# When GpSimd weighs two tiles of an expert layer: after a fixed pair step of the scans, or as soon as they are centred

## The chip, the core and the metric

One core of a Trainium2 chip runs the whole program. The metric is the time of one execution on the device, in microseconds (us); less is better. Five engines work side by side, each on its own list of instructions in order: TensorE (PE: matrix products and transposes), VectorE (DVE), ScalarE (ACT), GpSimd (POOL) and the queue of SyncE (SP), which starts transfers. They wait for one another through semaphores only. GpSimd starts the indirect transfers (gathers) too.

## What is computed

The program is two layers of a recurrent model. The part that matters here is the first: on the same normed input, a Mamba block (a scan over 512 positions) and a mixture of 24 experts with two choices for each token. The experts' first product is combined, layer-normed, passed through a relu, and goes into the experts' second product.

```
# Mamba: 8 sequences of 512, 256 channels, 16 states
h = dA * h + dBx          # a scan along the sequence, for each of 16 states
y = sum over states of h * C
# experts: W1 is 128 to 512, W2 512 to 128
h = moe_apply(xf, combine, dispatch, W1, b1)
h = layer_norm(h, lw, lb)   # lw, lb: one vector of 512 for each of 4 groups
h = relu(h)
return moe_apply(h, combine, dispatch, W2, b2)
```

## The kernel before, in words

Tokens lie in 32 tiles of 128 rows. The scan stage runs the Mamba scans as main work and the experts' work beside it: on each engine a function (side_by_side) takes a piece of the main list and then a piece of the other in turn, so the order of both on an engine is fixed when the program is written.

Main work: 64 pair steps, numbered 0 to 63, eight for each of eight sequences. Pair step i treats two states of 256 channels. TensorE spreads rows of B and C over 128 partitions in PSUM (L653, tile sc_p_bc). VectorE then does four products of 128x1024, two with B (L783) and two with C for the step before (L793); each has one input in SBUF and one in PSUM. Then it does two scans (L811, tensor_tensor_scan, 128x1024), whose two inputs, the decays sc_dA and the states sc_st, both lie in SBUF; each scan adds one to the semaphore scanned. Position q = i mod 8 in a sequence decides some extra work: at q = 3 and q = 6 the scans are followed by four short operations of the softplus for the next sequence (L760, L763, L764, L766, 128x512), whose inputs lie in SBUF, and the last adds one to u_ready. ScalarE makes the decays (L596), TensorE sums the states (L684).

Beside it, in steps 22 to 42, the combination of the first expert layer is done, two tiles (one unit u of 16) for each pair step:

- GpSimd gathers two rows of the experts' first product for each token of a tile: two gathers a tile (L1434, into the buffer yk of four tiles). The gather of tile t waits until tile t-4 has been combined (semaphore biased).
- TensorE adds a bias (L1528) and the two gathered rows (L1532) in a PSUM bank of two.
- ScalarE copies the bank out (L1655), works out mean and variance in a number of small instructions, and in its turn for unit u centres and scales unit u-2 (L1643, buffer ro of six tiles; semaphore centred) after it did the relu of unit u-4 (L1636), which waits for GpSimd.
- GpSimd weighs a unit: it multiplies the two centred tiles (128x1024) with the norm's weight (L1454) and adds the norm's bias (L1456), both in SBUF (semaphore weighted). All stands in one list: the gathers of tiles 2u+2 and 2u+3, then the weighing of unit u-3, and so on. The gathers come to an end with tile 31; units 12 to 15 are weighed without gathers between them.
- SyncE stores each unit after the relu, and when all is stored GpSimd gathers for the second expert layer (L1464).

Two waits stand ahead of a weighing: centred, and that of wait_window: unit u is weighed after the scans of pair step 25+u (scanned at 2 * (26+u)), or, where that step is at q = 3 or 6, after the softplus behind its scans (u_ready).

Of the kernel before, what the change touches and what calls it, by code (L numbers as in the profile page):

```python
# [29 lines left out]
DI, DS, DTR, KC = 256, 16, 8, 4  # L30
# [175 lines left out]
def front_stage(nc, w, src_dram, xn_dram, x_rows, xn_rows, xnT, xT, z, pt, routing, early, late, first,  # L206
# [3 lines left out]
    with ExitStack() as ctx:  # L210
# [74 lines left out]
        @block.gpsimd  # L285
        def _(pool):
            pool.wait_ge(stored, 16 * B)
            pool.wait_ge(turned, B)
            nc.gpsimd.memset(zero_rows, 0.0).then_inc(zeroed, 1)
            pool.wait_ge(routing.tab_ready, 1)  # L290
            pool.wait_ge(gates_stored, 16)
            for e in range(Moe0Experts.AHEAD):
                for h in range(HG):
                    nc.gpsimd.indirect_dma_start(
                        out=xg[:, e, h, :], out_offset=None, in_=xn_dram.rearrange("p t d -> (p t) d"),
                        in_offset=bass.IndirectOffsetOnAxis(ap=r.tab[:, h, e:e + 1], axis=0),
                    ).then_inc(gathered1[e], 16)
# [185 lines left out]
EVEN_FROM, EVEN_TO, FIRST_WINDOW = 22, 43, 26  # L483
# [7 lines left out]
def scan_stage(nc, w, xT, z, spare, first, beside):  # L491
# [6 lines left out]
    with ExitStack() as ctx:  # L498
# [338 lines left out]
        @block.gpsimd  # L837
        def _(pool):
            for _ in beside.pool(pool):
                pass  # L840
# [465 lines left out]
class Moe0Experts:  # L1306
# [108 lines left out]
    def pool(self, pool):  # L1415
        nc, r = self.nc, self.r

        def gather_x(e):
            if e >= E0:
                return  # L1420
            if e >= 4:
                pool.wait_ge(self.piece_read, 5 * (e - 3))
            for h in range(HG):
                nc.gpsimd.indirect_dma_start(  # L1424
                    out=self.xg[:, e % 4, h, :], out_offset=None, in_=self.xn_rows,
                    in_offset=bass.IndirectOffsetOnAxis(ap=r.tab[:, h, e:e + 1], axis=0),
                ).then_inc(self.gathered1[e % 4], 16)

        def gather_y(u):
            for t in range(2 * u, min(2 * u + 2, NT)):  # L1430
                if t >= 4:
                    pool.wait_ge(self.biased, t - 3)
                for k in range(2):
                    nc.gpsimd.indirect_dma_start(  # L1434
                        out=self.yk[:, t % 4, k, :], out_offset=None, in_=self.y1_rows,
                        in_offset=bass.IndirectOffsetOnAxis(ap=r.back[:, k, t:t + 1], axis=0),
                    ).then_inc(self.gathered_y[t % 4], 16)

        def wait_window(i):

            b, q = divmod(i - 1, DS // 2)
            if q in (3, 6):
                pool.wait_ge(self.u_ready, 2 * (b + 1) + (q - 3) // 3 + 1)
            else:
                pool.wait_ge(self.scanned, 2 * i)

        def weigh(u):

            pool.wait_ge(self.centred, 2 * u + 2)
            wait_window(FIRST_WINDOW + u)  # L1450
            t = 2 * u
            ro = self.ro[:, t % 6:t % 6 + 2, :]
            g = slice(t % HG, t % HG + 2)
            nc.gpsimd.tensor_tensor(ro, ro, self.w["ln_w"][:, g, :], ALU.mult).then_inc(self.p_chain, 1)  # L1454
            pool.wait_ge(self.p_chain, u + 1)
            nc.gpsimd.tensor_tensor(ro, ro, self.w["ln_b"][:, g, :], ALU.add).then_inc(self.weighted, 1)  # L1456

        def gather_r(e):
            if e >= E0:
                return  # L1460
            if e >= 3:
                pool.wait_ge(self.turned2, HG * (e - 2))
            for h in range(HG):
                nc.gpsimd.indirect_dma_start(  # L1464
                    out=self.rg[:, e % 3, h, :], out_offset=None, in_=self.r_rows,
                    in_offset=bass.IndirectOffsetOnAxis(ap=r.tab[:, h, e:e + 1], axis=0),
                ).then_inc(self.gathered2[e % 3], 16)

        for e in range(E0):
            gather_x(e + self.AHEAD)  # L1470
            yield
        for i in range(2):
            pool.wait_ge(self.stored1[i], 16 * (E0 // 2))
        gather_y(0)
        yield
        for u in range(self.UNITS + 4):
            gather_y(u + 1)
            if 3 <= u < self.UNITS + 3:
                weigh(u - 3)
            yield  # L1480
        for i in range(3):
            pool.wait_ge(self.stored_r[i], 16 * len(range(i, self.UNITS, 3)))
        for e in range(self.AHEAD):
            gather_r(e)
        yield
        for e in range(E0):
            gather_r(e + self.AHEAD)
            yield
# [1529 lines left out]
```

## Time and profile before

| | us |
|---|---|
| median of 3 runs | 1442.43 (1440.59 to 1442.75) |
| the profiled execution | 1438.98 |
| its span, first to last instruction | 1436.1 |
| scans of the first layer (L811), first to last start | 108.4 to 772.6 |
| units weighed (L1454), first to last start | 371.8 to 551.3 |

Busy time over the whole span: TensorE 1258.3 us (88%), VectorE 1199.1 (83%), ScalarE 883.8 (62%), GpSimd 681.2 (47%). These are means over stages of different kinds; for this change the stretch from 360 to 560 us counts. All times in this text are us from the start of the span. The timeline lists an engine's instructions by start, duration and, in brackets, the idle time of the engine ahead of it and what ended it. A duration includes time in which the instruction was held up after its start.

### The profile page before, as it was taken

The page shows a single profiled execution, that of the slowest core. Times are in us where ns is not written, and L with a number is a line of the kernel's source. Part 1 is how long each engine was busy: PE and PEld are TensorE (multiplying, and loading weights), DVE is VectorE, ACT ScalarE, POOL GpSimd, SP SyncE. Part 2 cuts the span into 40 slices and gives each one's busy share as a digit, 9 for nine tenths or more (in the row PEclk, how much of TensorE's full clock was granted, in tenths as well). Part 3 has the DMA queues.
Part 4 walks back from the last instruction along what each step waited for, and adds up shares of the span by engine and source line. Part 5 has one row for each costly group of instructions (what it writes and reads, how often), then busy time and mean ns, then how long its engine had stood idle before and what let it go on. Part 6 is the DMA issues. An engine that isn't in the chain of part 4 may idle for free. (4 is left out here: it accounts for less than half of the span.)

```text
span 1436.1 us, 21390 instructions
## 1 busy us (share of the span) xinstructions
PE 1258.3 (88%) x7254; PEld 874.3 (61%) x7260; DVE 1199.1 (83%) x2410; ACT 883.8 (62%) x2114; POOL 681.2 (47%) x633
## 2 busy tenths in 40 slices
PE   6988798887988865999897997799999999999997
PEld 5444354443443433888896775467667777777775
DVE  6868999998888889999996778688898755568876
ACT  5577667575988885556553657756456444544462
POOL 0026565615688855655651775338640143146300
PEclk9999999999889977999998899899999999999999
DMA  8014555455233422445552721010002044213200
GB/s 257 1 24 114 144 144 155 130 142 150 90 107 128 133 74 84 136 138 142 163 146 61 235 53 37 15 42 4 1 2 59 7 111 127 62 33 49 28 29 31
DMA packets 86021, 128.82 MB, mean 90 GB/s; under 512 B 15488, under 2 KB 50657, under 8 KB 85306
## 3 DMA queue, kind: packets, MB, share of 16 engines
q1 hardware_dynamic: 66458, 75.70, 18.0%
q0 software_dynamic: 19456, 51.77, 14.0%
q8 instruction: 58, 0.95, 0.3%
q14 instruction: 49, 0.40, 0.1%
HBM read 86.66 MB, written 40.77 MB: 89 GB/s over the span
## 5 line engine op out<-in xcount | busy, mean ns | idle before, releaser
L811 DVE TENSOR_TENSOR_SCAN sc_st<-sc_dA,sc_st 128x1024 f32<-128x1024 f32 x128 | 291.0, 2317 | 0.0
L2359 DVE COPY at_pT<-at_p_t 128x512 f32<-128x512 f32 (+1 forms) x192 | 108.8, 599 | 105.2 <-PE at_p_t L2136 105.0
L793 DVE TENSOR_TENSOR sc_st<-sc_st,sc_p_bc 128x1024 f32<-128x1024 f32 x128 | 155.7, 1217 | 31.6 <-PE sc_p_bc L653 31.5
L596 ACT ACTIVATE sc_dA<-sc_dt,g_state 128x511 f32<-128x511 f32 x256 | 168.8, 709 | 6.2 <-DVE sc_st L811 5.5
L783 DVE TENSOR_TENSOR sc_st<-sc_u,sc_p_bc 128x1024 f32<-128x1024 f32 x128 | 155.1, 1212 | 7.5 <-PE sc_p_y L684 6.5
L1464 POOL DMA_INDIRECT g_state<-r_scratch,moe_tab x96 | 122.2, 1273 | 82.0 <-PE e_bank L1560 55.2
L1424 POOL DMA_INDIRECT g_state<-xn_scratch,moe_tab x88 | 117.5, 1335 | 84.3 <-ACT g_state L1584 48.1
L2232 ACT ACTIVATE at_pr<-at_pr,at_nmx 128x512 f32<-128x512 f32 (+3 forms) x256 | 140.2, 552 | 23.3 <-DVE at_nmx L2318 23.2
L2116 PE MATMUL at_p_s<-g_xT,at_qT 128*128 128x512 f32 (+3 forms) x512 | 149.4, 435 | 0.0
L653 PE MATMUL sc_p_bc<-sc_bc,mamba_sel 96*128 96x512 bf16 x256 | 102.4, 401 | 51.3 <-DVE sc_st L783 47.4
L684 PEld LDWEIGHTS sc_p_y<-g_ident,sc_st 128*128 128x128 f32 x1024 | 121.7, 144 | 27.5 <-issue 14.1
L684 PE MATMUL sc_p_y<-g_ident,sc_st 128*128 128x128 f32 x1024 | 136.1, 277 | 2.0 <-DVE sc_st L793 1.9
L1434 POOL DMA_INDIRECT g_state<-y_scratch,moe_back x64 | 93.1, 1455 | 56.8 <-DMA y_scratch<-g_state 32.3
L2318 DVE CUSTOM_DVE_ANT_0 at_pr<-at_p_s,l_mask_wide 128x512 f32<-128x512 f32 (+3 forms) x256 | 110.4, 486 | 6.0 <-PE at_p_s L2116 5.5
L2116 PEld LDWEIGHTS at_p_s<-g_xT,at_qT 128*128 128x128 f32 x512 | 83.0, 191 | 50.2 <-issue 32.1
L1513 PE MATMUL e_bank<-g_state 128*96 128x512 f32 x192 | 99.0, 614 | 10.7 <-ACT g_state L1574 10.6
L1547 PE MATMUL e_bank<-g_state 128*96 128x128 f32 x768 | 101.7, 276 | 4.4 <-ACT g_state L1675 4.0
L1584 ACT ACTIVATE g_state<-e_bank,g_state 96x512 f32<-96x512 f32 x96 | 65.0, 680 | 62.1 <-PE e_bank L1513 60.3
L2136 PEld LDWEIGHTS at_p_t<-g_ident,at_pr 128*128 128x128 f32 x640 | 74.8, 141 | 43.0 <-DVE at_pT L2359 31.5
L2136 PE MATMUL at_p_t<-g_ident,at_pr 128*128 128x128 f32 x640 | 91.6, 274 | 6.9 <-DVE at_pT L2359 6.0
L1684 ACT ACTIVATE g_state<-e_bank 128x384 f32<-128x384 f32 x96 | 46.8, 487 | 77.7 <-PE e_bank L1560 77.6
L2570 POOL DMA_INDIRECT f_m<-y_scratch,l_back x64 | 60.4, 943 | 71.7 <-DMA y_scratch<-f_out 33.4
(343 smaller groups left out, 2718.9 us busy)
## 6 DMA issues: line engine op xcount, KB each, us to landing
y_scratch<-g_state SPq DMA_DIRECT2D x24, 768.0 KB, 5.2
g_state<-W SPq DMA_DIRECT2D x48, 256.0 KB, 5.5
r_scratch<-g_state SPq DMA_DIRECT2D x16, 512.0 KB, 2.6
y_scratch<-g_state SPq DMA_DIRECT2D x24, 192.0 KB, 2.7
xn_scratch<-g_state SPq DMA_DIRECT2D x16, 256.0 KB, 4.2
g_state<-x SPq DMA_DIRECT2D x4, 512.0 KB, 7.0
g_state<-xn_scratch SPq DMA_DIRECT2D x8, 256.0 KB, 5.8
g_state<-x SPq DMA_DIRECT2D x1, 2048.0 KB
```

Source lines behind the costliest of these rows:

```text
L596: ins = nc.scalar.activation(dA[:, m % 4, j, 1:L], dt[:, b % 2, h, 1:L], ACT.Exp, scale=negA[:, h, 2 * q + j:2 * q + j + 1])
L684: ins = nc.tensor.matmul(p_y[:, t, h * P:(h + 1) * P], st[:, m + h, j, t * P:(t + 1) * P], w["ident"], is_transpose=True, start=False, sto ...
L783: nc.vector.tensor_tensor(st[:, m % RS:m % RS + 2, j, :], u[:, b % 2, :, :], p_bc[:, k % 3, :].unsqueeze(1).broadcast_to([P, HALF, L]), AL ...
L793: nc.vector.tensor_tensor(states, states, p_bc[:, k % 3, :].unsqueeze(1).broadcast_to([P, HALF, L]), ALU.mult).then_inc(row_used, 1)
L811: nc.vector.tensor_tensor_scan(st[:, m % RS, :, :].rearrange("p a b -> p (a b)"), dA[:, m % 4, :, :].rearrange("p a b -> p (a b)"), st[:, ...
L1424: nc.gpsimd.indirect_dma_start(out=self.xg[:, e % 4, h, :], out_offset=None, in_=self.xn_rows, in_offset=bass.IndirectOffsetOnAxis(ap=r.ta ...
L1464: nc.gpsimd.indirect_dma_start(out=self.rg[:, e % 3, h, :], out_offset=None, in_=self.r_rows, in_offset=bass.IndirectOffsetOnAxis(ap=r.tab ...
L2116: ins = nc.tensor.matmul(p_s[:, bank, c:c + K], qT[:, n % 3, i * P:(i + 1) * P], xaT[:, b, 0:K], start=True, stop=True)
L2136: ins = nc.tensor.transpose(p_t[:, bank, c + (i - j) * P:c + (i - j + 1) * P], pr[:, n % 3, sbank, sc + j * P:sc + (j + 1) * P], w["ident"])
L2232: ins = nc.scalar.activation(row, row, ACT.Exp, scale=-1.0, bias=nmx[:, n % 2, i:i + 1], accum_out=sums[:, n % 4, i:i + 1])
L2318: ins = v.tensor_tensor_reduce(out=pr[:, n % 3, bank, c:c + K], in0=p_s[:, bank, c:c + K], in1=w["mask_wide"][:, L - K:L], scale=1.0, scal ...
L2359: v.tensor_copy(pT[:, n % 2, part, 0:cols], p_t[:, PT_BANK[part], 0:cols]).then_inc(pT_ready, 1)
```

## The change

The function wait_window and its call in weigh are taken away. Nothing else is changed: no instruction, no order.

```
-        def wait_window(i):
-
-            b, q = divmod(i - 1, DS // 2)
-            if q in (3, 6):
-                pool.wait_ge(self.u_ready, 2 * (b + 1) + (q - 3) // 3 + 1)
-            else:
-                pool.wait_ge(self.scanned, 2 * i)
-
         def weigh(u):
 
             pool.wait_ge(self.centred, 2 * u + 2)
-            wait_window(FIRST_WINDOW + u)
             t = 2 * u
```

GpSimd's list before, at the gathers of one unit and the two weighings around them (g_state is the arena in which ro and yk lie, e_ the expert part, sc_ the scan part):

```order
L1454 TENSOR_TENSOR g_state<-g_state,moe_ln_w 128x1024 [waits sc_scanned,e_centred]
L1456 TENSOR_TENSOR g_state<-g_state,moe_ln_b 128x1024 [waits e_p_chain]
L1434 DMA g_state<-y_scratch,moe_back 128x512 [waits e_biased]
L1434 DMA g_state<-y_scratch,moe_back 128x512
L1434 DMA g_state<-y_scratch,moe_back 128x512 [waits e_biased]
L1434 DMA g_state<-y_scratch,moe_back 128x512
L1454 TENSOR_TENSOR g_state<-g_state,moe_ln_w 128x1024 [waits sc_u_ready,e_centred]
L1456 TENSOR_TENSOR g_state<-g_state,moe_ln_b 128x1024 [waits e_p_chain]
```

And in the changed kernel, where all lines behind are nine less:

```order
L1445 TENSOR_TENSOR g_state<-g_state,moe_ln_w 128x1024 [waits e_centred]
L1447 TENSOR_TENSOR g_state<-g_state,moe_ln_b 128x1024 [waits e_p_chain]
L1434 DMA g_state<-y_scratch,moe_back 128x512 [waits e_biased]
L1434 DMA g_state<-y_scratch,moe_back 128x512
L1434 DMA g_state<-y_scratch,moe_back 128x512 [waits e_biased]
L1434 DMA g_state<-y_scratch,moe_back 128x512
L1445 TENSOR_TENSOR g_state<-g_state,moe_ln_w 128x1024 [waits e_centred]
L1447 TENSOR_TENSOR g_state<-g_state,moe_ln_b 128x1024 [waits e_p_chain]
```

The order is the same; the waits for sc_scanned and sc_u_ready are gone from the multiplication, and e_centred and, on the gathers, e_biased are left.

GpSimd's list before, at the last gather and the units 12 to 14, which follow one another:

```order
L1434 DMA g_state<-y_scratch,moe_back 128x512
L1454 TENSOR_TENSOR g_state<-g_state,moe_ln_w 128x1024 [waits sc_scanned,e_centred]
L1456 TENSOR_TENSOR g_state<-g_state,moe_ln_b 128x1024 [waits e_p_chain]
L1454 TENSOR_TENSOR g_state<-g_state,moe_ln_w 128x1024 [waits sc_scanned,e_centred]
L1456 TENSOR_TENSOR g_state<-g_state,moe_ln_b 128x1024 [waits e_p_chain]
L1454 TENSOR_TENSOR g_state<-g_state,moe_ln_w 128x1024 [waits sc_u_ready,e_centred]
L1456 TENSOR_TENSOR g_state<-g_state,moe_ln_b 128x1024 [waits e_p_chain]
```

And in the changed kernel:

```order
L1434 DMA g_state<-y_scratch,moe_back 128x512
L1445 TENSOR_TENSOR g_state<-g_state,moe_ln_w 128x1024 [waits e_centred]
L1447 TENSOR_TENSOR g_state<-g_state,moe_ln_b 128x1024 [waits e_p_chain]
L1445 TENSOR_TENSOR g_state<-g_state,moe_ln_w 128x1024 [waits e_centred]
L1447 TENSOR_TENSOR g_state<-g_state,moe_ln_b 128x1024 [waits e_p_chain]
L1445 TENSOR_TENSOR g_state<-g_state,moe_ln_w 128x1024 [waits e_centred]
L1447 TENSOR_TENSOR g_state<-g_state,moe_ln_b 128x1024 [waits e_p_chain]
```

Here no gather stands between two weighings, so that only e_centred parts them.

## Rows read from the trace of the kernel before

**Rows 1.** Busy time by stretch, columns: stretch, length, each engine, PEclk, DMA.

```profile
385.00:515.00 130.00, 110.72 (x363) 51.23 (x362) 104.91 (x76) 113.97 (x311) 116.07 (x62) 0.87 0.40 125
515.00:560.00 45.00, 27.17 (x119) 17.29 (x118) 44.06 (x33) 31.85 (x69) 18.87 (x9) 0.77 0.15 59
560.00:780.00 220.00, 198.77 (x1683) 178.44 (x1682) 216.20 (x157) 126.16 (x233) 122.20 (x96) 0.98 0.49 133
```

**Rows 2.** Timeline of GpSimd, one round: start, us, operation, idle before.

```profile
440.72 2.79 POOL L1434 DMA_INDIRECT g_state<-y_scratch,moe_back  x1 [0.15 <-issue]
443.81 1.84 POOL L1434 DMA_INDIRECT g_state<-y_scratch,moe_back  x1 [0.30 <-issue]
...
447.21 0.95 POOL L1434 DMA_INDIRECT g_state<-y_scratch,moe_back  x1 [0.30 <-issue]
448.17 2.36 POOL L1454 TENSOR_TENSOR g_state<-g_state,moe_ln_w 128x1024 f32<-128x1024 f32 x1
450.61 2.35 POOL L1456 TENSOR_TENSOR g_state<-g_state,moe_ln_b 128x1024 f32<-128x1024 f32 x1
453.10 2.91 POOL L1434 DMA_INDIRECT g_state<-y_scratch,moe_back  x1
```

**Rows 3.** Groups by line, 360 to 560 us: busy, mean ns, idle before, releasers.

```profile
L811 DVE TENSOR_TENSOR_SCAN sc_st<-sc_dA,sc_st 128x1024 f32<-128x1024 f32 x35 | 83.1, 2413 | 0.0
...
L793 DVE TENSOR_TENSOR sc_st<-sc_st,sc_p_bc 128x1024 f32<-128x1024 f32 x34 | 41.3, 1214 | 21.6 <-PE sc_p_bc L653 21.6
...
L783 DVE TENSOR_TENSOR sc_st<-sc_u,sc_p_bc 128x1024 f32<-128x1024 f32 x34 | 41.1, 1210 | 4.2 <-PE sc_p_y L684 4.2
...
L1454 POOL TENSOR_TENSOR g_state<-g_state,moe_ln_w 128x1024 f32<-128x1024 f32 x16 | 38.2, 2387 | 34.3 <-DVE sc_st L811 24.1 <-DVE sc_u L766 10.1
...
L1636 ACT ACTIVATE g_state<-g_state 128x1024 f32<-128x1024 f32 x16 | 16.9, 1053 | 26.1 <-POOL g_state L1456 26.1
```

**Rows 4.** Timeline of GpSimd: the first two tiles weighed.

```profile
371.80 2.79 POOL L1454 TENSOR_TENSOR g_state<-g_state,moe_ln_w 128x1024 f32<-128x1024 f32 x1 [10.01 <-DVE sc_st L811]
```

**Rows 5.** Timeline of VectorE: scans of steps 26, 28, 37 (x2 merges two), a wait.

```profile
376.92 4.46 DVE L811 TENSOR_TENSOR_SCAN sc_st<-sc_dA,sc_st 128x1024 f32<-128x1024 f32 x2
...
388.81 1.22 DVE L793 TENSOR_TENSOR sc_st<-sc_st,sc_p_bc 128x1024 f32<-128x1024 f32 x1 [4.05 <-PE sc_p_bc L653]
...
403.20 4.47 DVE L811 TENSOR_TENSOR_SCAN sc_st<-sc_dA,sc_st 128x1024 f32<-128x1024 f32 x2
...
515.54 4.47 DVE L811 TENSOR_TENSOR_SCAN sc_st<-sc_dA,sc_st 128x1024 f32<-128x1024 f32 x2
```

**Rows 6.** Timelines of GpSimd and VectorE: a weighing beside scans of step 29.

```profile
412.13 4.38 POOL L1456 TENSOR_TENSOR g_state<-g_state,moe_ln_b 128x1024 f32<-128x1024 f32 x1
...
412.09 6.58 DVE L811 TENSOR_TENSOR_SCAN sc_st<-sc_dA,sc_st 128x1024 f32<-128x1024 f32 x2
```

**Rows 7.** Timelines of VectorE and GpSimd in the next stage: short two-input operations.

```profile
873.65 1.37 DVE L1844 TENSOR_TENSOR g_xT<-g_xT,g_state 128x256 f32<-128x256 f32 x1
...
877.63 0.43 DVE L1844 TENSOR_TENSOR g_xT<-g_xT,g_state 128x256 f32<-128x256 f32 x1
...
873.43 1.31 POOL L1791 TENSOR_TENSOR g_xT<-g_xT 128x512 f32<-128x512 f32 x1
```

**Rows 8.** Timeline of GpSimd: units 12 and 13, without gathers.

```profile
520.15 2.35 POOL L1454 TENSOR_TENSOR g_state<-g_state,moe_ln_w 128x1024 f32<-128x1024 f32 x1 [5.11 <-DVE sc_st L811]
...
532.74 2.36 POOL L1454 TENSOR_TENSOR g_state<-g_state,moe_ln_w 128x1024 f32<-128x1024 f32 x1 [7.81 <-DVE sc_u L766]
```

**Rows 9.** Timeline of VectorE: scans of step 38 and the softplus behind them.

```profile
525.37 4.47 DVE L811 TENSOR_TENSOR_SCAN sc_st<-sc_dA,sc_st 128x1024 f32<-128x1024 f32 x2
529.75 0.67 DVE L760 SCALAR_TENSOR_TENSOR g_state<-g_state,sc_logs 128x512 f32<-128x512 f32 x1
```

**Rows 10.** Timeline of ScalarE: centring of unit 14, and its wait for unit 13.

```profile
526.49 1.50 ACT L1643 ACTIVATE g_state<-g_state,e_nm,e_rstd 128x512 f32<-128x512 f32 x2
...
537.56 1.06 ACT L1636 ACTIVATE g_state<-g_state 128x1024 f32<-128x1024 f32 x1 [4.07 <-POOL g_state L1456]
```

## The prediction

> **What bounds the kernel now.** I read the busy times by stretch first, since the shares over the whole span mix stages. From 560 to 780 us VectorE is busy 216.2 of 220 us, from 515 to 560 it is busy 44.06 of 45; from 385 to 515 only 104.91 of 130, while GpSimd is busy 116.07 and ScalarE 113.97 [rows 1]. So VectorE's scans pace the stage, except in the stretch where gathers and weighings share GpSimd. There one round of GpSimd is four gathers and a weighing, without a gap: from the gather at 440.72 to that at 453.10 are 12.38 us [rows 2]. VectorE's steps keep the same pace: from the scans of step 26 at 376.92 to those of step 37 at 515.54 are 138.62 us for 11 steps, 12.60 each [rows 5]. What GpSimd is late with reaches VectorE through TensorE and ScalarE: VectorE waits 21.6 us ahead of L793 and 4.2 us ahead of L783, and ScalarE waits 26.1 us for weighings ahead of its relu [rows 3]. The waits removed are the two releasers of L1454, 24.1 and 10.1 us, in 8 of its 16 instructions [rows 3]; the first alone is 10.01 us, from 361.79 to 371.80 [rows 4].
>
> **What the wait did beside waiting.** Scans and weighings hold each other up. At 412.13 the second operation of a weighing took 4.38 us instead of 2.35, and the two scans that began at 412.09 took 6.58 instead of 4.47 [rows 2, 5, 6]: the first scan ran 2.2 us, then the weighing 2.35 while the second scan stood, then the second scan. So a weighing operation that comes while the first scan runs costs VectorE 2.1 to 2.35 us, one that comes in the second scan costs it nothing, and one that is under way when the first scan wants to begin costs the rest of itself. Short operations with both inputs in SBUF suffer alike: a TENSOR_TENSOR of 128x256 took 1.37 us beside a GpSimd operation of the same kind that began at 873.43 and took 1.31, and 0.43 alone [rows 7]. The four products of a step, with one input in PSUM, are not held: their mean over the whole stretch with its weighings is 1.21 us [rows 3]. The gathers are held too, but hold nobody: 2.79 and 1.84 us beside scans, 0.95 alone [rows 2], and the scans beside them stay at 4.46 or 4.47 [rows 5].
>
> The last point is where a page speaks otherwise. The Trainium skill (SBUF — State Buffer, Who interferes with whom) says that a VectorE tensor_tensor with two SBUF inputs contends with GpSimd's reads and infers that the making of DMA descriptors is not held by it. By that a round of GpSimd would be 2.73 us shorter (1.84 and 0.89 less), 9.65 us, and GpSimd would not be the bound before. The trace disagrees, if a scan counts as such an instruction, and I go by the rows.
>
> **The sum, part by part.** No instruction goes or comes, so everything lies in when weighings run. Behind the multiplication in GpSimd's list stand the addition and the next unit's gathers; who waits for these are ScalarE's relu and TensorE's L1532.
>
> *1. Removed waits, steps 26 to 37.* The first weighing begins at 361.79 instead of 371.80 (its tiles were centred long before: the wait named is the scans), and later ones lose the short waits for softplus. The two long waits of these last units, 5.11 and 7.81 us [rows 8], are not in this part. At best GpSimd ends its last gather 10.0 us earlier, and some 2 us more for three short waits inside the rounds (10.1 - 7.81 = 2.3 [rows 3, 8]): a bound of -12.3 us, if no collision is added.
>
> *2. Added collisions, steps 26 to 37.* I walk the first rounds. A weighing from 361.8 to 366.7, four gathers in 7.4 us beside the scans of step 25, then the next weighing from 374.2 to 379.0 (two operations at 2.44, 2.35 each). The scans of step 26, wanted at 376.92, start at 379.0: 2.1 lost. They end at 383.4; the four products take 4.5, so step 27 wants its scans at 387.9. GpSimd's gathers, held by the scans, end at 386.6, its first operation runs to 389.0: 1.1 lost; the first scan runs to 391.3, the second operation to 393.6, the second scan stands 2.35. Then softplus and products lead to 403.2, where the next weighing is in its second half, to 405.4: 2.2 lost. Three steps have lost 7.75 us, 2.6 a step, and the wait of 4.05 at 388.81 and a shorter one are gone. Step 28's scans, at 403.20 before, come at 405.4. Over the twelve steps 26 to 37 that is 12 x 2.6 = 31 us, against the 25.8 us of waits (21.6 + 4.2) and the collisions that before has already (83.1 us for 35 scans [rows 3], where 35 of 4.47 / 2 are 78.2: 4.9), together 30.7. I take **0** for parts 1 and 2 together. The bounds: -12.3 as above, and +8 if the kernel falls into the pattern that alternates at every step: products, half a weighing waited for (1.75), scan, weighing (2.35), scan, which is 9.0 + 4.1 = 13.1 a step against 12.6, so 6 us in 11 steps and the 2 of the start. I stay near the middle, since the walk of three rounds is the nearest that I have.
>
> *3. The tail, units 12 to 15.* Before, each waited for its window, 5.11, 7.81 and 9.0 us for the last two (24.1 - 10.01 - 5.11) [rows 3, 4, 8], and cost VectorE at most 0.4. Here VectorE is the bound with nothing to win, and nothing slows GpSimd: 4.9 us a unit. Unit 12 follows unit 11 at about 515: its first operation comes between the scans of step 37, +2.35. Unit 13 starts near 524.8, its first half holds the first scan of step 38 by 0.4 and its second half comes between the two scans, +2.35; the wait of 0.8 that stood ahead of step 38 goes. Unit 14, whose tiles are centred by 528.0 [rows 10], comes in the second scan and then beside the softplus behind step 38. Its four short operations, 0.7 us each [rows 9], need one another in turn, so GpSimd can take its turn ahead of each: two operations of unit 14 and two of unit 15, 4 x 2.35 = +9.4. Unit 15 is there for it, since the centring of 15 stood behind a relu that waited 4.07 us for unit 13 [rows 10], and that now is weighed by 532. Sum: 2.35 + 0.4 - 0.8 + 2.35 + 9.4 = **+13.7 us**. What is least sure is the 9.4: no row shows four such turns in a row, only the one of rows 7. From below it is 0 (the softplus done before unit 14 gets in), from above 9.4.
>
> Behind step 38 no weighing is left to collide, the lateness stays: VectorE has 3.8 us of air in the 220 us to the stage's end [rows 1], and the next stage starts when this one ends. Total 0 + 13.7 = +13.7 us, on the profiled execution 1438.98 + 13.7 = 1452.7. The median of the runs before is 3.45 us above that execution, so 1442.43 + 13.7 = **1456.1 us**.
>
> **The rivals.**
> - *The change as walked, tail and all*: 1456, from 1450 to 1464 (the pattern of every step adds 8). For it: each single collision has its row. Against it: the times of the tail depend on ScalarE's turn to 1 or 2 us. Chance 0.58.
> - *The tail misses the softplus*: ScalarE centres 15 later, or unit 14 is through before. Then 2.35 + 0.4 - 0.8 + 2.35 = +4.3, 1446.7, with part 2 at 0 to +3. Chance 0.16.
> - *Faster: GpSimd's head start is kept.* The mechanism is the round: GpSimd is the one without a gap, and collisions cost VectorE time that it had spare anyway, as long as they stay under 25.8 us in the twelve steps, 2.15 a step. If they come to 1.5 a step, GpSimd's 12.3 are kept in large part: about -12 in these steps, +4.3 in the tail, -8: 1434.7. ScalarE's own work allows it (113.97 busy in 130 us, so 11.0 a step). Chance 0.16.
> - *Nothing changes*: half of the weighings (8 of 16) did not wait for the window at all [rows 3], and the others might find their phase by themselves, since the gathers are held by the scans and so put the weighing behind them. Then within 3 us of 1442.4. Chance 0.10.
>
> **How the numbers follow.** 0.2% is 2.9 us, about what a measurement of this kernel can tell from no change. Slower: 0.58, most of the second rival (0.15), together 0.74. Same: 0.10. Faster: 0.16. The range leaves out the faster rival's better half and the worst pattern at every step together with a full tail: 1437 to 1465.
>
> **What would show it.** In the changed kernel L1454 waits for no scan; its first instruction starts near 361.8. The scans (L811) have a sum about 30 us above 83.1 in the stretch, with pairs of 6.6 to 8 us instead of 4.47. VectorE's 21.6 us ahead of L793 shrink below 12, and ScalarE's 26.1 below 8. The scans of step 37 start within some us of 515.5, those of step 39 about 14 us after 537; L760 to L766 behind step 38 take 10 to 12 us in all. It would be wrong if step 37 came by 508 already, if the scans kept 4.47 beside weighings, or if the lateness at 560 shrank by the stage's end.

## The result, and the profile after

| | before | changed |
|---|---|---|
| median, us | 1442.59 (1440.59 to 1445.08, 4 runs) | 1459.15 (1457.42 to 1460.3, 4 runs) |
| ratio to before | | 1.0114, 95% interval 1.0088 to 1.0141 |
| span of the profiled execution | 1436.1 | 1457.4 |

The changed kernel is slower by 16.6 us, 1.1%. Of the 21.3 us between the two profiled spans not all belongs to the change: the scans of step 24, ahead of the first weighing, begin at 356.56 in the one trace and at 360.78 in the other, and in the traces of the experiments below at 360.1 to 362.6. So I compare traces by the time since the scans of step 24: to those of step 37, with which the rounds of gathers end, and to those of step 42, behind which both kernels run the same way.

| us from the scans of step 24 | before | changed | difference |
|---|---|---|---|
| to step 37 | 158.98 | 167.95 | +9.0 |
| to step 42 | 210.46 | 228.16 | +17.7 |

The busy times by stretch, in the changed kernel (columns: stretch, length, TensorE, its weight loads, VectorE, ScalarE, GpSimd, clock, DMA share):

```profile
385.00:515.00 130.00, 106.02 (x329) 49.04 (x327) 128.75 (x72) 109.11 (x299) 118.49 (x59) 0.84 0.38 118
515.00:575.00 60.00, 32.16 (x131) 17.91 (x130) 59.90 (x36) 35.93 (x84) 34.48 (x11) 0.76 0.12 44
575.00:795.00 220.00, 200.24 (x1667) 178.87 (x1667) 218.05 (x159) 127.82 (x234) 125.24 (x96) 0.96 0.49 135
```

VectorE is busy 128.75 of 130 us between 385 and 515, against 104.91 before [rows 1]: it has no idle time left, and yet is slower. What fills it is time in which its instructions are held. The groups by line show that, from 360 to 575 us:

```profile
L811 DVE TENSOR_TENSOR_SCAN sc_st<-sc_dA,sc_st 128x1024 f32<-128x1024 f32 x34 | 118.1, 3513 | 0.0
...
L1447 POOL TENSOR_TENSOR g_state<-g_state,moe_ln_b 128x1024 f32<-128x1024 f32 x16 | 62.7, 3916 | 1.3
...
L1445 POOL TENSOR_TENSOR g_state<-g_state,moe_ln_w 128x1024 f32<-128x1024 f32 x16 | 42.5, 2654 | 4.4 <-ACT g_state L1634 4.1
L793 DVE TENSOR_TENSOR sc_st<-sc_st,sc_p_bc 128x1024 f32<-128x1024 f32 x34 | 41.2, 1211 | 0.0
L783 DVE TENSOR_TENSOR sc_st<-sc_u,sc_p_bc 128x1024 f32<-128x1024 f32 x33 | 39.9, 1208 | 0.9 <-PE sc_p_y L684 0.9
...
L1627 ACT ACTIVATE g_state<-g_state 128x1024 f32<-128x1024 f32 x16 | 16.7, 1045 | 0.9 <-POOL g_state L1447 0.8
```

The waits of before are gone: 21.6 us ahead of L793 are 0, the 4.2 us ahead of L783 are 0.9, and the 26.1 us that ScalarE waited for weighings are 0.8 [rows 3]. In their place the 34 scans take 118.1 us, 3513 ns each, where 35 took 83.1 and 2413 ns (rows 3 are of 360 to 560 us). GpSimd's second operation (L1447, the old L1456) takes 3916 ns in the mean.

The pattern of the rounds, on both engines. GpSimd first, then VectorE, start and duration in front:

```profile
366.11 2.38 POOL L1445 TENSOR_TENSOR g_state<-g_state,moe_ln_w 128x1024 f32<-128x1024 f32 x1
...
380.41 2.38 POOL L1445 TENSOR_TENSOR g_state<-g_state,moe_ln_w 128x1024 f32<-128x1024 f32 x1
...
393.81 2.36 POOL L1445 TENSOR_TENSOR g_state<-g_state,moe_ln_w 128x1024 f32<-128x1024 f32 x1
396.25 4.23 POOL L1447 TENSOR_TENSOR g_state<-g_state,moe_ln_b 128x1024 f32<-128x1024 f32 x1
...
409.91 4.34 POOL L1447 TENSOR_TENSOR g_state<-g_state,moe_ln_b 128x1024 f32<-128x1024 f32 x1
```

```profile
381.14 8.11 DVE L811 TENSOR_TENSOR_SCAN sc_st<-sc_dA,sc_st 128x1024 f32<-128x1024 f32 x2
...
393.67 8.96 DVE L811 TENSOR_TENSOR_SCAN sc_st<-sc_dA,sc_st 128x1024 f32<-128x1024 f32 x2
402.55 0.66 DVE L760 SCALAR_TENSOR_TENSOR g_state<-g_state,sc_logs 128x512 f32<-128x512 f32 x1
...
409.82 6.58 DVE L811 TENSOR_TENSOR_SCAN sc_st<-sc_dA,sc_st 128x1024 f32<-128x1024 f32 x2
```

The first weighing stands at 366.11 with no wait ahead of it, 5.3 us after the scans of step 24 (before: 15.2). The pair of scans of step 27 takes 8.96 us instead of 4.47. The start of the first scan is recorded 0.14 us before that of GpSimd's multiplication, and yet the multiplication takes 2.36 us, as alone, and the pair takes two of GpSimd's operations longer: multiplication, scan, addition (4.23 us, held by the scan), scan. The next pair starts 16.15 us later, behind the softplus, at 409.82, together with GpSimd's addition, and takes 6.58 us. From step 26 to step 37 the pairs come 13.42 us apart in the mean, and GpSimd's multiplications of units 1 to 11 (380.41 to 515.37) 13.50 us. Between 385 and 515 us GpSimd waits 1.1 us for another engine and VectorE 0.9, so the two meet again at every step: of the twelve pairs none takes under 6.5 us, and four take 8.96.

The tail, GpSimd and then VectorE:

```profile
530.17 3.04 POOL L1445 TENSOR_TENSOR g_state<-g_state,moe_ln_w 128x1024 f32<-128x1024 f32 x1 [1.25 <-ACT g_state L1634]
533.29 4.22 POOL L1447 TENSOR_TENSOR g_state<-g_state,moe_ln_b 128x1024 f32<-128x1024 f32 x1
540.34 3.86 POOL L1445 TENSOR_TENSOR g_state<-g_state,moe_ln_w 128x1024 f32<-128x1024 f32 x1 [2.83 <-ACT g_state L1634]
544.27 4.21 POOL L1447 TENSOR_TENSOR g_state<-g_state,moe_ln_b 128x1024 f32<-128x1024 f32 x1
548.44 2.79 POOL L1445 TENSOR_TENSOR g_state<-g_state,moe_ln_w 128x1024 f32<-128x1024 f32 x1
551.31 2.67 POOL L1447 TENSOR_TENSOR g_state<-g_state,moe_ln_b 128x1024 f32<-128x1024 f32 x1
```

```profile
528.73 6.62 DVE L811 TENSOR_TENSOR_SCAN sc_st<-sc_dA,sc_st 128x1024 f32<-128x1024 f32 x2
...
539.79 6.56 DVE L811 TENSOR_TENSOR_SCAN sc_st<-sc_dA,sc_st 128x1024 f32<-128x1024 f32 x2
546.27 2.76 DVE L760 SCALAR_TENSOR_TENSOR g_state<-g_state,sc_logs 128x512 f32<-128x512 f32 x1
549.07 2.71 DVE L763 TENSOR_TENSOR g_state<-sc_logs,g_state 128x512 f32<-128x512 f32 x1
551.81 2.71 DVE L764 TENSOR_TENSOR sc_dt<-sc_dt,g_state 128x512 f32<-128x512 f32 x1
554.56 0.69 DVE L766 TENSOR_TENSOR sc_u<-sc_dt,g_xT 128x512 f32<-128x512 f32 x1
...
559.69 4.47 DVE L811 TENSOR_TENSOR_SCAN sc_st<-sc_dA,sc_st 128x1024 f32<-128x1024 f32 x2
```

The pairs of steps 37 and 38 take 6.62 and 6.56 us. Three of the four short softplus operations behind step 38 take 2.7 to 2.8 us instead of 0.69, each ending about 0.55 us behind one of GpSimd's operations of units 14 and 15, so that it ran when that had ended; the fourth is alone.

### The profile page after: what moved, and what is told of

It reads as the page before. It is cut to its first block and busy times, and to the rows that moved or that the text cites. A ratio compares the mean times of both kernels' runs of the same rounds, so it can differ in the third digit from the quotient of the medians.

```text
span 1457.4 us, 21380 instructions
## 1 busy us (share of the span) xinstructions
PE 1266.4 (87%) x7260; PEld 878.6 (60%) x7260; DVE 1241.6 (85%) x2410; ACT 883.8 (61%) x2114; POOL 708.6 (49%) x633
## 5 line engine op out<-in xcount | busy, mean ns | idle before, releaser
L811 DVE TENSOR_TENSOR_SCAN sc_st<-sc_dA,sc_st 128x1024 f32<-128x1024 f32 x128 | 328.2, 2607 | 0.0
L596 ACT ACTIVATE sc_dA<-sc_dt,g_state 128x511 f32<-128x511 f32 x256 | 169.1, 710 | 19.3 <-DVE sc_st L811 11.8
L653 PE MATMUL sc_p_bc<-sc_bc,mamba_sel 96*128 96x512 bf16 x256 | 103.4, 405 | 87.1 <-DVE sc_st L783 83.1
L1455 POOL DMA_INDIRECT g_state<-r_scratch,moe_tab x96 | 125.2, 1305 | 102.7 <-PE e_bank L1551 54.9
L793 DVE TENSOR_TENSOR sc_st<-sc_st,sc_p_bc 128x1024 f32<-128x1024 f32 x128 | 155.5, 1216 | 9.6 <-PE sc_p_bc L653 9.5
L783 DVE TENSOR_TENSOR sc_st<-sc_u,sc_p_bc 128x1024 f32<-128x1024 f32 x128 | 155.0, 1211 | 5.1 <-PE sc_p_y L684 3.2
L1434 POOL DMA_INDIRECT g_state<-y_scratch,moe_back x64 | 89.6, 1400 | 56.9 <-DMA y_scratch<-g_state 32.4
L1504 PE MATMUL e_bank<-g_state 128*96 128x512 f32 x192 | 99.9, 620 | 12.3 <-ACT g_state L1565 12.2
L653 PEld LDWEIGHTS sc_p_bc<-sc_bc,mamba_sel 96*128 96x128 bf16 x256 | 25.9, 101 | 129.7 <-DVE sc_st L783 106.3
```

What stands on the lines that cost most here:

```text
L596: ins = nc.scalar.activation(dA[:, m % 4, j, 1:L], dt[:, b % 2, h, 1:L], ACT.Exp, scale=negA[:, h, 2 * q + j:2 * q + j + 1])
L653: nc.tensor.matmul(p_bc[:, k % 3, :], w["sel"][:, n * P:(n + 1) * P], bc3[:, b % 2, :], start=True, stop=True).then_inc(row_ready, 1)
L783: nc.vector.tensor_tensor(st[:, m % RS:m % RS + 2, j, :], u[:, b % 2, :, :], p_bc[:, k % 3, :].unsqueeze(1).broadcast_to([P, HALF, L]), AL ...
L793: nc.vector.tensor_tensor(states, states, p_bc[:, k % 3, :].unsqueeze(1).broadcast_to([P, HALF, L]), ALU.mult).then_inc(row_used, 1)
L811: nc.vector.tensor_tensor_scan(st[:, m % RS, :, :].rearrange("p a b -> p (a b)"), dA[:, m % 4, :, :].rearrange("p a b -> p (a b)"), st[:, ...
L1455: nc.gpsimd.indirect_dma_start(out=self.rg[:, e % 3, h, :], out_offset=None, in_=self.r_rows, in_offset=bass.IndirectOffsetOnAxis(ap=r.tab ...
```

## The experiments

The theory: the loss is that a GpSimd operation reading SBUF and a VectorE instruction with two inputs there exclude each other, so that the removed wait's worth was to keep weighings beside the four products. Against it stand, part by part: that all of the loss is in the tail (my sum), that it is GpSimd's time or the order of its work, and that it comes from the head start alone. The wait's condition is changed in six kernels, the weighing itself in two. The table gives each run's measured ratio, the difference of the medians and, from its one trace, the time since step 24 against before. Where a ratio is turned into us below, it is taken of the median before; the differences of the medians are up to 2.2 us away from that. Two traces of the same kernel (first_free) are 4.7 us apart at step 37, so a difference of a few us between two traces shows nothing by itself.

| kernel | units that wait | median, us | ratio to before, 95% | medians' difference | to step 37 | to step 42 |
|---|---|---|---|---|---|---|
| changed | none | 1459.15 | 1.0114 (1.0088 to 1.0141) | +16.6 | +9.0 | +17.7 |
| tail_kept | 12 to 15 | 1450.84 | 1.0051 (1.0032 to 1.0070) | +9.4 | +8.9 | +8.4 |
| tail_free | 0 to 11 | 1452.41 | 1.0061 (1.0040 to 1.0082) | +10.9 | -1.1 | +10.7 |
| first_kept | 0 | 1450.00 | 1.0046 (1.0025 to 1.0067) | +8.5 | -5.3 | +6.7 |
| first_free | 1 to 15 | 1437.71 | 0.9967 (0.9945 to 0.9988) | -3.8 | -7.9 | -7.1 |
| first_free_again | 1 to 15 | 1437.65 | 0.9963 (0.9941 to 0.9984) | -5.2 | -3.2 | -3.6 |
| middle_free | 0, 12 to 15 | 1439.32 | 0.9983 (0.9964 to 1.0002) | -2.7 | -4.9 | -4.1 |
| second_kept | 1, 12 to 15 | 1436.35 | 0.9963 (0.9937 to 0.9988) | -6.5 | -8.8 | -8.1 |
| softplus_kept | 2, 5, 10, 13 | 1444.97 | 1.0017 (0.9999 to 1.0036) | +3.0 | -1.2 | +5.6 |
| write_only | none, reads nothing | 1420.78 | 0.9865 (0.9836 to 0.9894) | -21.2 | -22.0 | -20.3 |
| no_weighing | no weighing | 1422.71 | 0.9869 (0.9840 to 0.9897) | -19.3 | -22.1 | -20.3 |

The kernel before ran beside each group: 1441.47 us (the first four experiments), 1441.99 (the next four in time: write_only, no_weighing, softplus_kept, middle_free), 1442.88 (the last two).

### Where the loss lies: rounds or tail

```
-            wait_window(FIRST_WINDOW + u)
+            if u >= 12:
+                wait_window(FIRST_WINDOW + u)
```

> The wait for the pair step is kept for units 12 to 15 and gone for units 0 to 11. My theory after the changed kernel's trace: the twelve steps with gathers cost 9 us of the 16.6, because scans and weighings alternate at 13.4 us a step instead of 12.6; so this is 9 us above the kernel before, near 1451.6 us. The rival, my own sum on record: these steps cost nothing (0) and all of it lies in the tail; then it equals the kernel before, 1442.6 us.

Measured: 0.51% above before, 7.4 us. Step 37 is reached as late as in the changed kernel, and from there nothing more is lost. VectorE's scans of steps 35 to 38 show the switch, two pairs beside weighings without wait and two behind them:

```profile
501.37 8.94 DVE L811 TENSOR_TENSOR_SCAN sc_st<-sc_dA,sc_st 128x1024 f32<-128x1024 f32 x2
...
517.51 6.58 DVE L811 TENSOR_TENSOR_SCAN sc_st<-sc_dA,sc_st 128x1024 f32<-128x1024 f32 x2
...
528.52 4.46 DVE L811 TENSOR_TENSOR_SCAN sc_st<-sc_dA,sc_st 128x1024 f32<-128x1024 f32 x2
...
537.41 4.85 DVE L811 TENSOR_TENSOR_SCAN sc_st<-sc_dA,sc_st 128x1024 f32<-128x1024 f32 x2
```

```
+            if u < 12:
+                wait_window(FIRST_WINDOW + u)
```

> The wait is kept for units 0 to 11 and gone for units 12 to 15. Theory: the tail costs 7 to 9 us, mostly by four short softplus operations behind step 38 that each wait for a weighing operation, so about 1450.5 us. My sum on record said 13.7 us, 1456.3. Rival: with units 0 to 11 at their old times, unit 15 does not meet the softplus and the tail costs only the scans' 4.3 us, 1446.9.

Measured: 0.61%, 8.8 us. Within what was measured the two parts add up: by the ratios 7.4 + 8.8 = 16.2 us against 16.6 for both, by the medians 9.4 + 10.9 = 20.3, by the traces at step 42 8.4 + 10.7 = 19.1 against 17.7; the intervals are 4.6 to 10.1 and 5.8 to 11.8 us. By the trace the tail is 11.8 us (10.7 + 1.1), more than in the changed kernel, because here all four softplus operations are held, one by each operation of units 14 and 15, 2.05 us each:

```profile
532.54 6.58 DVE L811 TENSOR_TENSOR_SCAN sc_st<-sc_dA,sc_st 128x1024 f32<-128x1024 f32 x2
539.03 2.77 DVE L760 SCALAR_TENSOR_TENSOR g_state<-g_state,sc_logs 128x512 f32<-128x512 f32 x1
541.83 2.71 DVE L763 TENSOR_TENSOR g_state<-sc_logs,g_state 128x512 f32<-128x512 f32 x1
544.58 2.71 DVE L764 TENSOR_TENSOR sc_dt<-sc_dt,g_state 128x512 f32<-128x512 f32 x1
547.33 2.72 DVE L766 TENSOR_TENSOR sc_u<-sc_dt,g_xT 128x512 f32<-128x512 f32 x1
549.96 1.21 DVE L783 TENSOR_TENSOR sc_st<-sc_u,sc_p_bc 128x1024 f32<-128x1024 f32 x1
```

The rival, that unit 15 misses the softplus, is refuted, and so is my sum's 0 for the rounds.

### Is it the head start

```
+            if u == 0:
+                wait_window(FIRST_WINDOW + u)
```

> Only unit 0 waits for its pair step, all others are free. Two theories on why steps 26 to 37 lose 9 us. If it is the head start of 10 us that puts GpSimd's rounds into the wrong phase, this kernel keeps the rhythm of before (8 of 16 weighings did not wait there anyway), loses only the tail's 8 us, and takes about 1450.5 us. If the alternating pattern draws every rhythm in that has no wait, it is as slow as the changed kernel, 1459 us.

Measured: 0.46%, 6.6 us, so not the 16.6 of the changed kernel: the alternating pattern does not draw in every rhythm. With one wait at the start the rounds reach step 37 even 5.3 us earlier than before, and the tail then loses 12.0. So the 9 us in the rounds come from the phase that the unwaited first weighing sets, together with the waits that are missing later: each alone does not bring them. Two kernels further on in the table narrow this down to a single wait each. middle_free is tail_kept with the wait of unit 0, and takes 1439.32 us where tail_kept took 1450.84; second_kept is tail_kept with the wait of unit 1, and takes 1436.35.

```
+            if u > 0:
+                wait_window(FIRST_WINDOW + u)
```

> Only unit 0 is free, units 1 to 15 keep the wait. Unit 0 fits between the gathers of tile 9 and the scans of step 25, where it collides with nothing, and the four gathers behind it come 10 us earlier; unit 1 then waits for step 26 and starts at its window, some 3.3 us earlier than in the kernel before (381.4 instead of 384.66). Theory: 3 us faster than before, 1439.6 us, since GpSimd's round of 12.4 us is the bound up to the last gather. Rival: the head start is lost at the first window, and the time is that of before, 1442.6.

Measured: 0.33% faster, and 0.37% in a second run of the same kernel. GpSimd's timeline shows the first weighing where the changed kernel has it, and the second at its window:

```profile
366.05 2.37 POOL L1455 TENSOR_TENSOR g_state<-g_state,moe_ln_w 128x1024 f32<-128x1024 f32 x1
...
385.69 2.36 POOL L1455 TENSOR_TENSOR g_state<-g_state,moe_ln_w 128x1024 f32<-128x1024 f32 x1 [5.36 <-DVE sc_st L811]
```

> The kernel in which only unit 0 is free, once more: it was 0.33% faster than the kernel before, with an interval from 0.12% to 0.55%. If the reason holds (the round of GpSimd is the bound up to the last gather, and its first weighing meets no scan), it is 0.2 to 0.5% faster again, 1435 to 1439 us; if it was chance, it equals the kernel before.

The rival is refuted: the head start is kept by the wait of unit 1, not lost there. The two traces differ (7.9 and 3.2 us at step 37), so a part of the gain depends on the execution. In the first of them GpSimd waits for VectorE only once between 385 and 515 us, those 5.36 us of unit 1: the waits of units 2 to 11 stand in the list and are always met already. In the second unit 5 waits 2.15 us and unit 10 0.78.

### Is it the reading of SBUF

```
-            nc.gpsimd.tensor_tensor(ro, ro, self.w["ln_w"][:, g, :], ALU.mult).then_inc(self.p_chain, 1)
-            pool.wait_ge(self.p_chain, u + 1)
-            nc.gpsimd.tensor_tensor(ro, ro, self.w["ln_b"][:, g, :], ALU.add).then_inc(self.weighted, 1)
+            for k in range(3):
+                nc.gpsimd.memset(ro, 0.5).then_inc(self.p_chain, 1)
+                pool.wait_ge(self.p_chain, 3 * u + k + 1)
+            nc.gpsimd.memset(ro, 0.5).then_inc(self.weighted, 1)
```

> The changed kernel, with each weighing (a multiplication and an addition that read and write 128x1024 in SBUF) replaced by four memsets of the same two tiles, which write SBUF and read nothing; so the norm's weight and bias of the first expert layer are left out and the relu's input is a constant. GpSimd is busy about as long. Theory: the loss is the reading of SBUF by GpSimd beside operations of VectorE with two inputs there; then the pairs of scans go back to about 4.5 us and the softplus operations to 0.7, and the time falls to 1435 to 1440 us. Rival: what is lost is GpSimd's time and order, or its writes hold the scans as well; then pairs of 6.6 to 9 us stay and the time is 1450 us or more.

Measured: 1.35% faster than before, 19.5 us, below what I expected. The groups by line, 355 to 575 us, and the stretch of the rounds:

```profile
L811 DVE TENSOR_TENSOR_SCAN sc_st<-sc_dA,sc_st 128x1024 f32<-128x1024 f32 x43 | 96.0, 2271 | 0.0
...
L1446 POOL MEMSET g_state<- 128x1024 f32 x48 | 45.9, 956 | 22.1 <-ACT g_state L1635 20.2
...
L1448 POOL MEMSET g_state<- 128x1024 f32 x16 | 15.2, 953 | 0.9
...
L764 DVE TENSOR_TENSOR sc_dt<-sc_dt,g_state 128x512 f32<-128x512 f32 x5 | 3.5, 692 | 0.2
```

```profile
385.00:515.00 130.00, 116.30 (x413) 56.98 (x412) 118.71 (x90) 129.24 (x356) 100.49 (x89) 0.89 0.41 129
```

64 memsets of 128x1024 lie among the scans (61.1 us together, 3.8 us a unit) and the scans take 2271 ns each, the softplus operations 692. Every single pair of steps 26 to 37 takes 4.46 or 4.47 us. The same SBUF is written, at no fixed time, and nothing of VectorE's is held (GpSimd's gathers still are, 1419 ns in the mean). So writing is not what holds the scans. That it is the reading is what is left, and not shown by itself: a memset differs from a weighing in its operation too, and no run reads without writing. The bound is then ScalarE, busy 129.24 of 130 us.

```
+            nc.gpsimd.memset(ro[:, 0, 0:1], 0.5).then_inc(self.weighted, 1)
```

> The changed kernel with the weighing left out: one memset of a single element for each unit stands for it (the norm's weight and bias are not applied). It shows what the stage takes when only the gathers are on GpSimd. A round is then some 7.5 us, so the bound goes to ScalarE, 11 us of work a step, and VectorE, 9.9: steps 26 to 37 at 11 us instead of 12.6 give 17 us less than before, 1425 us, and every pair of scans takes 4.5 us though the gathers run beside them. If the gathers hold the scans too, pairs over 4.5 us stay.

```profile
L811 DVE TENSOR_TENSOR_SCAN sc_st<-sc_dA,sc_st 128x1024 f32<-128x1024 f32 x43 | 96.1, 2273 | 0.0
L1434 POOL DMA_INDIRECT g_state<-y_scratch,moe_back x50 | 69.7, 1393 | 62.8 <-PE e_bank L1521 49.2 <-issue 13.6
```

```profile
385.00:515.00 130.00, 115.27 (x415) 56.79 (x414) 119.09 (x89) 129.27 (x359) 52.83 (x50) 0.91 0.40 125
```

Measured: 1.31% faster, 18.9 us: the same as with the memsets (to step 37, 137.0 and 136.9 us), though GpSimd is busy 52.83 us in the stretch and not 100.49. So GpSimd's time is not what costs, in the absence of its reads. The scans take 2273 ns beside 50 gathers of 1393 ns: gathers are held by scans, and scans not by gathers.

### Scans or softplus

```
+            if (FIRST_WINDOW + u - 1) % 8 in (3, 6):
+                wait_window(FIRST_WINDOW + u)
```

> The wait is kept only for units 2, 5, 10 and 13, whose window lies behind a softplus, and gone for the other twelve. If the cost of the change is mostly in the softplus operations, this is near the kernel before, 1442 to 1445 us. If it is the scans, the alternating pattern is broken only four times: 3 to 6 us are won against the changed kernel in steps 26 to 37, and units 14 and 15 may still meet something in the tail: 1446 to 1453 us. I expect the second.

```profile
L811 DVE TENSOR_TENSOR_SCAN sc_st<-sc_dA,sc_st 128x1024 f32<-128x1024 f32 x37 | 100.0, 2741 | 0.0
...
L763 DVE TENSOR_TENSOR g_state<-sc_logs,g_state 128x512 f32<-128x512 f32 x4 | 2.8, 692 | 0.1
```

Measured: 0.17%, 2.5 us over before, the interval reaches down to 0.9999; the median, 1444.97, lies in the range of the first of the two answers, and I had expected the second. Four waits of sixteen save 14 of the 16.6 us. But they do more than guard the softplus: the time that scans are held in steps 26 to 37 falls from 40.0 us to 12.8 as well, since each wait sets the phase anew. So this kernel does not part the two causes; the tail's traces do: 8.2 us of softplus in tail_free (4 x 2.05).

### The rounds without waits, the tail with them

```
+            if u == 0 or u >= 12:
+                wait_window(FIRST_WINDOW + u)
```

> Unit 0 and units 12 to 15 wait, units 1 to 11 are free. The trace with only unit 0 waiting reached step 37 5.3 us earlier than the kernel before (counted from step 24) and lost 11.9 us behind it. If both hold apart from each other, this kernel keeps the 5.3 us and loses nothing in the tail: 1436 to 1437 us. Rival: the 5.3 us were one execution's luck in phase; then it is the kernel before, 1441.5 us.

Measured: 0.17% faster, interval to 1.0002; the trace has -4.9 us at step 37 and -4.1 at step 42. Neither theory can be dropped by the time alone. Two softplus operations in the rounds, at 400.71 and 437.65, were held for a whole multiplication of GpSimd; the second:

```profile
437.65 3.00 DVE L766 TENSOR_TENSOR sc_u<-sc_dt,g_xT 128x512 f32<-128x512 f32 x1
```

```profile
437.75 2.35 POOL L1455 TENSOR_TENSOR g_state<-g_state,moe_ln_w 128x1024 f32<-128x1024 f32 x1
```

```
+            if u == 1 or u >= 12:
+                wait_window(FIRST_WINDOW + u)
```

> Units 1 and 12 to 15 wait, units 0 and 2 to 11 are free. Unit 0 alone free was 4.8 us faster than the kernel before, and units 1 to 11 free 2.5 us. If both add up, this takes about 1435 us, 6 to 7 us less than before. Rival: what the rhythm of the free rounds wins depends on the phase in which it starts, so it can fall into the alternating pattern at 13.4 us a step as in the changed kernel; then 1446 us or more.

Measured: 0.37% faster (interval 0.9937 to 0.9988), as first_free in both its runs (0.33% and 0.37%). It is faster than the kernel before and the changed kernel; that units 2 to 11 are free adds nothing that can be measured, which fits the trace of first_free, where their waits never held GpSimd. The sum of the two gains, which I expected, did not come by the ratio (5.3 us) and came by the medians (6.5 us), so it stays open. One of the twelve runs took 1450.06 us, the others 1430.3 to 1442.5; it has no trace, so it can't be told whether that one fell into the slow pattern. What first_free and second_kept share is the best of what was run: unit 0 without the wait, unit 1 and the tail with it.

## Why the prediction was right, and where it was not

Forecast was 1456.1 us, +13.7 us; measured are 1459.15 and +16.6 us. The direction, the mechanism and the size hold; the division between the parts does not.

1. *The wait's removal moves the first weighing.* As predicted: 5.3 us after the scans of step 24 begin, where it had been 15.2, and nothing waited for. The waits of VectorE and ScalarE that I counted as the gain fell by more than I said: 25.8 us to 0.9 ahead of L793 and L783, 26.1 to 0.8 ahead of the relu.
2. *Added collisions, steps 26 to 37: the term that was mis-sized.* I took 2.6 us a step from a walk of three rounds, 31 us in twelve steps, and set them against 30.7 of waits and old collisions, so 0. In the trace the twelve pairs take 40.0 us more than 12 x 4.47, 3.3 a step, and step 37 is 9.0 us late. My 30.7 were taken from 360 to 560 us; counted in both traces from step 24 to the start of step 37, the scans are held 37.9 us against 4.1 and VectorE's waits are 0.9 against 25.0, which gives 9.7. So the form of the account was right and its input, the collisions of a step, wrong.
   - What the walk missed: it had 2.1, 3.45 and 2.2 us at steps 26, 27 and 28, 7.75 together; the trace has 3.64, 4.49 and 2.11, 10.24 together. Behind the first weighing I took 7.4 us for four gathers, and they took 9.3, since one of them was held for 5.57 over both scans of step 25. So the next weighing began 2 us later against the scans of step 26 and cost them the rest of its multiplication and its whole addition. At step 27 both engines come within 0.2 us, and where I had the scan lose 1.1 us to the first operation, it loses the whole 2.2.
   - What the account left out: the collisions cost GpSimd as well. Its additions take 3916 ns in the mean instead of 2350 alone, and units 1 to 11 come 13.50 us apart, where they came 12.56 apart before. So a head start of 9.9 us at unit 0 (5.3 instead of 15.2 us behind the scans of step 24) is gone at unit 11, which comes 154.6 us behind them instead of 153.7. The bound of -12.3 took the old round as given.
   - The upper bound, an alternation at every step, was 13.1 us a step and +8 (11 x 0.5 is 5.5 and not 6, so +7.5); the trace has 13.4 and +9.0. The nearness is in part luck: the bound has 9.0 us of own work a step and 4.1 of collisions, the trace 10.0, since softplus and other short operations belong to it, and 3.4. I chose the middle, and the trace landed at the end.
3. *The tail: 13.7 predicted, 9.5 us from the scans of step 37 to those of step 39* (30.96 against 21.50). The 2.35 at step 37 was 2.15, and it was unit 13's multiplication that came between these scans, not unit 12's, which had begun at 522.12, 6.6 us ahead of them. Step 38 lost 2.1, to the multiplication of unit 14, and not 2.35 + 0.4 to unit 13. The wait of 0.8 went as said. The softplus lost 3 x 2.05 = 6.15 us and not 9.4: GpSimd waited 2.83 us for the centring of unit 14, which I had taken as ready: rows 10 show it done by 528.0 before, but here ScalarE's list is late as well and ends it at 540.26. So its multiplication came between the two scans of step 38, and three operations instead of four were left. Sum 2.15 + 2.1 - 0.84 + 6.15 = 9.6. 0.7 us came back behind it, where two pairs had taken 4.8 us beside the last weighings before and take 4.47 now: 17.7 at step 42 instead of 18.4.
4. *Lateness stays.* From 575 to 795 us VectorE is busy 218.05 of 220.
5. The two errors, +9.0 in the rounds and -4.2 in the tail, partly cancel. That the total, 13.7 forecast and 16.6 measured, came so near is luck in that part. (The chances for slower, 0.58 and 0.15, add up to 0.73 and not 0.74.)

On the rivals: the faster one needed collisions under 2.15 us a step, they were 3.3. Its mechanism is real all the same: with the waits kept from unit 1 on, collisions in the rounds are 7.0 us in the twelve steps (first_free) and the head start is kept. The Trainium skill infers that the making of descriptors is not held by a tensor_tensor with two inputs in SBUF (SBUF — State Buffer, Who interferes with whom); the changed kernel's trace disagrees as well, as far as a scan is such an instruction: a gather of 5.57 us stands at 371.08 beside the scans of step 25. The other rule of the Trainium skill there, that a GpSimd operation which only writes is not in the way of VectorE's two inputs, is what write_only shows: 2271 ns a scan.

## What to carry to other kernels

A wait that looks like lost time on an engine can be the thing that keeps two engines off a shared resource; ahead of taking it away, look at which instructions then run together, what that costs both engines, and whether the other engine's idle time is worth more than what they cost each other. Two periodic lists of nearly the same length without a wait between them can fall into a bad phase and stay in it; here one wait near the start, of unit 0 or of unit 1, was enough for a good one. Where only the first of a row of waits has nothing to guard, it alone can go: 0.3 to 0.4% here.

## What was not expected

- The order at a close start: a scan whose start is recorded 0.14 us before a GpSimd multiplication still let it go first (393.67 and 393.81, pair 8.96 us), and so did a softplus operation recorded 0.10 us before one (middle_free, 437.65 and 437.75). It is not so for the addition, which follows the multiplication at once: recorded 0.09 us behind a scan it was held for it (409.82 and 409.91, pair 6.58 us, addition 4.34). In the traces of the kernel before, the changed kernel, tail_kept, tail_free, first_kept, middle_free and softplus_kept every multiplication recorded 0.08 to 0.15 us behind a scan or a softplus operation went first, and every addition recorded 0.04 to 0.12 us behind a scan went second. What decides it stays open.
- A gather issued 0.3 us before a pair of scans was held over both of them:

```profile
371.08 5.57 POOL L1434 DMA_INDIRECT g_state<-y_scratch,moe_back  x1 [0.16 <-issue]
376.95 0.95 POOL L1434 DMA_INDIRECT g_state<-y_scratch,moe_back  x1 [0.30 <-issue]
```

  The next one took 0.95. In the kernel before a gather began 0.35 us before the pair of step 27, at 389.94, and took 0.98, and in write_only one took 5.21 that began 0.01 us behind the start of the scans of step 25, so what decides it stays open. The row of before:

```profile
389.59 0.98 POOL L1434 DMA_INDIRECT g_state<-y_scratch,moe_back  x1
```

- Sixty-four memsets of 128x1024 on GpSimd (0.95 us each) in the place of the weighings cost the kernel nothing over having none at all: 1420.78 and 1422.71 us, with intervals that overlap.
- All weighings together, with their waits or collisions, cost about 20 us of the kernel before. That nearly all of it is exclusion, and next to nothing GpSimd's time as such, is likely and not shown: the memsets of a unit take 3.8 us, and a weighing alone 4.7. An estimate from write_only speaks for it: GpSimd still waits 16.3 us for the centring between 385 and 515 us there, in about 12 rounds, so 0.9 us more a round would find room.
